# Cross-attention: the value products of a batch packed in one PSUM bank, with one flip per batch; division and row scaling moved to GpSimd

## The reference

```
xn  = layernorm(x)                         # rows scaled: (x - mean) * rstd
q   = rmsnorm_per_head(xn @ Wq.T)          # 32 heads of 8 columns
k   = rmsnorm_per_head(ctx @ Wk.T)
v   = ctx @ Wv.T
p   = softmax(q k^T / sqrt(8))             # per head, 128 x 128
x  += concat_heads(p @ v)
```

## Time and profile before

| | before |
|---|---|
| median of three runs | 487.55 us (486.32 to 487.72) |
| span of the profiled execution | 485.7 us |
| PE busy | 422.1 us (87%) |
| DVE busy | 347.6 us (72%) |
| ACT busy | 175.4 us (36%) |
| POOL busy | 60.0 us (12%) |
| stage C, first scores to first product of stage D | 349.72 to 445.67 us |

### The profile page before, as it was taken

How to read it: one execution, slowest core, us unless ns; L and a number is a source line. 1 busy time by engine, 2 the same in 40 slices (tenths; PEclk the granted TensorE clock), 3 DMA queues, 4 the chain that set the end, 5 groups by cost and what they waited for, 6 DMA issues and landing times.

```text
span 485.7 us, 8153 instructions
## 1 busy us (share of the span) xinstructions
PE 422.1 (87%) x2754; PEld 264.6 (54%) x2754; DVE 347.6 (72%) x948; ACT 175.4 (36%) x230; POOL 60.0 (12%) x132
## 2 busy tenths in 40 slices
PE   5269998999999987999999999999878777596896
PEld 4125554555555543366666667677556555364444
DVE  7895888888887858466545626676876777868693
ACT  1105444455454451233343433343354444341001
POOL 3222324233242110000000000000000000000000
PEclk9777999999999998999999999999998889876997
DMA  6552335466364031000000000233125554630011
GB/s 214 151 164 70 97 118 158 133 216 196 121 197 123 4 118 43 0 2 0 1 0 0 1 1 11 62 90 111 53 78 164 163 160 126 180 89 1 1 43 43
DMA packets 63408, 42.53 MB, mean 88 GB/s; under 512 B 4625, under 2 KB 61201, under 8 KB 63377
## 3 DMA queue, kind: packets, MB, share of 16 engines
q1 hardware_dynamic: 62080, 41.24, 28.4%
q10 hardware_dynamic: 1296, 0.89, 0.7%
HBM read 27.76 MB, written 14.16 MB: 86 GB/s over the span
## 4 chain that ended last, share of the span: by engine, by line
issue 52%; PE 23%; DVE 14%; POOL 4%; DMA 3%; SPq 1%; ACT 1%; POOLq 0%; DVEq 0%
PE psum L501 7%; PE psum L469 3%; PE psum L489 3%; DVE mx L1114 3%; PE psum L456 2%; PE psum L816 2%; POOL parts L315 1%; PE psum L800 1%; DVE stats L1089 1%; PE psum L587 1%; DMA qstk<-mT 1%; DMA wa<-in_wa 1%; PE psum L725 1%; DVE rope_ab L1103 1%; DMA kstk<-stack_scratch 1%
## 5 line engine op out<-in xcount | busy, mean ns | idle before, releaser
L857 ACT ACTIVATE prob<-psum 128x1024 f32<-128x1024 f32 x64 | 65.6, 1024 | 89.8 <-PE psum L489 89.7
L1114 DVE TENSOR_REDUCE mx<-psum 128x2 f32<-128x512 f32 x128 | 84.1, 682 | 17.9 <-PE psum L469 16.9
L1334 DVE SCALAR_TENSOR_TENSOR xall<-psum,comb,xall 128x256 f32<-128x256 f32 x128 | 53.1, 477 | 41.5 <-PE psum L612 41.1
L612 PE MATMUL psum<-wdn,act 128*128 128x256 f32 x320 | 75.5, 379 | 0.6 <-DVE xall L1331 0.6
L599 PE MATMUL psum<-xnT,wup 128*128 128x512 f32 x160 | 76.0, 598 | 0.0
L612 PEld LDWEIGHTS psum<-wdn,act 128*128 128x128 f32 x320 | 60.7, 190 | 25.9 <-issue 19.1
L501 PE MATMUL psum<-prob,vt 128*32 128x256 f32 x512 | 69.0, 389 | 0.7 <-DVE pvT L1128 0.5
L900 ACT ACTIVATE rel<-psum 128x512 f32<-128x512 f32 x40 | 23.9, 597 | 96.2 <-PE psum L599 96.2
L469 PE MATMUL psum<-kstk,qstk 128*128 128x256 bf16 x256 | 50.8, 283 | 3.4 <-DVE mx L1114 3.3
L315 POOL TENSOR_TENSOR parts<-qk_rest,parts 128x512 bf16<-128x512 f32 x15 | 17.3, 1156 | 244.2 <-ACT parts L925 236.5
L958 ACT ACTIVATE prob<-psum 128x1024 f32<-128x1024 f32 x32 | 32.7, 1024 | 31.4 <-PE psum L710 30.4
(11 more groups left out here) (149 smaller groups left out, 484.7 us busy)
## 6 DMA issues: line engine op xcount, KB each, us to landing
qstk<-stack_scratch SPq DMA_DIRECT2D x32, 256.0 KB, 3.2
kstk<-stack_scratch SPq DMA_DIRECT2D x64, 128.0 KB, 3.3
stack_scratch<-parts SPq DMA_DIRECT2D x32, 192.0 KB, 2.3
stack_scratch<-parts SPq DMA_DIRECT2D x32, 128.0 KB, 2.2
wup<-in_wup SPq DMA_DIRECT2D x4, 640.0 KB, 4.8
wdn<-in_wdn SPq DMA_DIRECT2D x4, 640.0 KB, 5.6
stack_scratch<-parts SPq DMA_DIRECT2D x32, 64.0 KB, 1.9
ctx<-in_ctx SPq DMA_DIRECT2D x10, 128.0 KB, 2.2
```

Of the source, the lines that this page charges most:

```text
L612: last = nc.tensor.matmul(y_banks(y)[:, j // 2, (j % 2) * D:(j % 2 + 1) * D], act2[n % 2][:, j * P:(j + 1) * P], wdn[:, BLOCKS[g], :], sta ...
L857: nc.scalar.activation(prob[k % 2][:], exp_buf(k).rearrange("p a n -> p (a n)"), ACT.Exp, scale=SCALE).then_inc(exp_done, 1)
L1114: nc.vector.tensor_reduce(mx[:, half, :, 4 * s + p4:4 * s + p4 + 1], bank.rearrange("n (b m) -> n b m", b=2), AX_X, ALU.max).then_inc(misc ...
L1334: last = nc.vector.scalar_tensor_tensor(out=xall[:, b, :], in0=src, scalar=comb[:, b, e:e + 1], in1=xall[:, b, :], op0=ALU.mult, op1=ALU.add)
```

## The change

In stage C the products of all four steps of a batch go to one PSUM bank (7). Each step owns 128 columns of it; its two groups of four heads (pp 0 and 1) are accumulated onto each other: the pitch of `vt` grows from 32 to 40 columns, the values move to columns 8 to 15, and the second group's weight is read from column 0 and the first's from column 8, so that the two groups' results lie in different rows of the same 32 partitions. The count of matmuls stays. DVE then flips a batch once (`flip_c`), takes the reciprocal of 32 sums at once, GpSimd does the division in four instructions (`divide_c`), and DVE flips back (`flip_back_c`). The flips of batch b-1 now stand in slot b: `flip_c` at spot 0, in front of `v`, and `flip_back_c` at spot 4. PE's wait on `pv_free` stands at step 0 alone. `normalize_c` moves from DVE to GpSimd, with the mean negated beforehand on DVE. `qkT` moves from spot 3 to spot 4 (behind the scores of step 3), `o` from spot 4 to spot 6. The scaling of q and k becomes one instruction of 512 columns. In stage A only the column slices of `vt` change.

```diff
@@ (tiles, semaphores)
-        vt = [sb(f"vt{i}", [P, 2, 16, 32]) for i in range(2)]
+        vt = [sb(f"vt{i}", [P, 2, 16, VROW]) for i in range(2)]        # VROW = 40
+        den_c = sb("den_c", [P, 32])
+        nmean = sb("nmean", [P, NB])
@@ c_uses
             u = [("v",)] if m and spot == 0 else []
-            u += [("qkT",)] if t and spot == 3 else []
-            u += [("o",)] if o and spot == 4 else []
+            u += [("qkT",)] if t and spot == 4 else []
             u += [("xT",)] if pqk and spot == 5 else []
             u += [("cT",)] if pqk and spot == 5 else []
+            u += [("o",)] if o and spot == 6 else []
             u += [("qk",)] if pqk and spot == 7 else []
@@ PE, pv_c
                 pe.wait_ge(exp_done, NB * PAIRS + b * C_STEPS + k + 2)
-                if k % 2 == 0:
-                    pe.wait_ge(pv_free, 2 * NB + 2 * b + k // 2 + 1)
+                if k == 0:
+                    pe.wait_ge(pv_free, 2 * NB + 2 + b)
                 v = vt[par][:].rearrange("m a h r -> m (a h) r")
                 for pp in range(2):
                     for j in range(4):
                         h = 4 * pp + j
-                        g = 2 * (k % 2) + pp
-                        last = nc.tensor.matmul(pv_bank(k // 2)[32 * j:32 * j + 32, g * P:(g + 1) * P],
-                                                v[:, 8 * k + h, :], prob[k % 2][:, h * P:(h + 1) * P],
-                                                start=True, stop=True)
+                        last = nc.tensor.matmul(pv_bank(1)[32 * j:32 * j + 32, k * P:(k + 1) * P],
+                                                v[:, 8 * k + h, 0:32] if pp else v[:, 8 * k + h, 8:40],
+                                                prob[k % 2][:, h * P:(h + 1) * P],
+                                                start=(pp == 0), stop=(pp == 1), skip_group_check=True)
@@ PE, stage D
-            pe.wait_ge(pv_free, 4 * NB + 2)
+            pe.wait_ge(pv_free, 3 * NB + 2)
@@ POOL
-            with pool.Fori(0, 4) as i:
-                for par in range(2):
-                    third(NB + 2 * i + par, par)
+            def normalize_c(b):
+                pool.wait_ge(stats_ready, b // 4 + 1)
+                nc.gpsimd.tensor_scalar(xn[b % 2][:], xall[:, b, :], nmean[:, b:b + 1], rstd[:, b:b + 1],
+                                        ALU.add, ALU.mult).then_inc(xn_ready, 1)
+            def divide_c(b):
+                pool.wait_ge(den_ready, b + 1)
+                pool.wait_ge(o3_ready, NB + b)
...
+                for k in range(4):
+                    last = nc.gpsimd.tensor_tensor(
+                        o[:, k // 2, k % 2], cells[:, k, :, 0:2 * HD].rearrange("p n (t d) -> p n t d", d=HD),
+                        by[:, k].unsqueeze(3).broadcast_to((P, 4, 2, HD)), ALU.mult)
+                last.then_inc(o2_ready, 1)
...
+            for b in range(NB):
+                flags = c_flags(b)
+                if b < NB - 3:
+                    xn_gone(c_base(b - 1) + c_index(c_flags(b - 1), ("xT",)) if b else
+                            B_END + C_PRO.index(("xT", 1)))
+                    normalize_c(b + 3)
+                if b:
+                    divide_c(b - 1)
+                if b < NB - 2:
+                    third(NB + b + 2, b % 2)
+            divide_c(NB - 1)
@@ DVE, c_use("qk")
-                    for ten in range(2):
-                        last = nc.vector.tensor_tensor(
-                            qkn[:, ten].rearrange("n (h d) -> n h d", d=HD),
-                            bank[:, ten * D:(ten + 1) * D].rearrange("n (h d) -> n h d", d=HD),
-                            rs[:, 32 * ten:32 * ten + 32].unsqueeze(2).broadcast_to((P, 32, HD)), ALU.mult)
-                    last.then_inc(misc_free, 1)
+                    nc.vector.tensor_tensor(qkn[:].rearrange("n t (h d) -> n (t h) d", d=HD),
+                                            bank.rearrange("n (h d) -> n h d", d=HD),
+                                            rs[:].unsqueeze(2).broadcast_to((P, 64, HD)), ALU.mult
+                                            ).then_inc(misc_free, 1)
@@ DVE, divide_c(b, i) goes, and in its place
+            def flip_c(b):
+                dve.wait_ge(pv_done, NB * PAIRS + b * C_STEPS + C_STEPS)
+                nc.vector.transpose(pvT[0][:], pv_bank(1)).then_inc(pv_free, 1)
+                dve.wait_ge(pv_free, 2 * NB + b + 3)
+                nc.vector.reciprocal(den_c[:].rearrange("p (x t) -> p x t", t=2),
+                                     pvT[0][:].rearrange("p (x r) -> p x r", r=32)[:, :, 2 * HD:2 * HD + 2]
+                                     ).then_inc(den_ready, 1)
+            def flip_back_c(b):
+                dve.wait_ge(o2_ready, b + 1)
+                nc.vector.transpose(o3[:], o2[:]).then_inc(o3_ready, 1)
@@ DVE, slot_c
-                if pqk:
-                    normalize(b + 3, (b0 + 1) % 2)
                 n = 0
                 for spot in range(2 * C_STEPS):
-                    if spot in (3, 7):
-                        divide_c(b, spot // 7)
+                    if spot == 0 and shape:
+                        flip_c(b - 1)
+                    if spot == 4 and shape:
+                        flip_back_c(b - 1)
@@ DVE, after the slots
+            flip_c(NB - 1)
...
             weigh(0)
+            flip_back_c(NB - 1)
             ring(("o",))
```

More of the change, by code:

```diff
@@ L28 @@
 MAX_ROW = 46
+VROW = 40
 PAIRS = 8
@@ L160, in build @@
         qk_ready = sem("qk_ready")
+        stats_ready = sem("stats_ready")
+        den_ready = sem("den_ready")
+        o2_ready = sem("o2_ready")
         hi_done = sem("hi_done")
@@ L502, in pv @@
                             pv_bank(1)[32 * j:32 * j + 32, (g % 2) * D:(g % 2 + 1) * D],
-                            vt[par][:, mb, 2 * k + s, :],
+                            vt[par][:, mb, 2 * k + s, 8:40],
                             prob[k % 2][:, (2 * s + mb) * D:(2 * s + mb + 1) * D],
@@ L1056, in _, with xn_gone @@
                 slot(b, 0, b)
-            with pool.Fori(0, 4) as i:
-                for par in range(2):
-                    third(NB + 2 * i + par, par)
+            def normalize_c(b):
[5 more added lines that the diff above has]
+                pool.wait_ge(o3_ready, NB + b)
+                cells = pvT[0][:].rearrange("p (k n r) -> p k n r", k=4, r=32)
+                o = o2[:].rearrange("p (i n k t d) -> p i k n t d", i=2, n=4, t=2, d=HD)
+                by = den_c[:].rearrange("p (k n t) -> p k n t", k=4, t=2)
+                for k in range(4):
[3 more added lines that the diff above has]
+                last.then_inc(o2_ready, 1)
+            def xn_gone(u):
+                pool.wait_ge(misc_free, u + 1)
+            for b in range(2):
+                normalize_c(b)
+            xn_gone(B_END + C_PRO.index(("xT", 0)))
+            normalize_c(2)
+            third(NB, 0)
+            third(NB + 1, 1)
+            for b in range(NB):
[9 more added lines that the diff above has]
+            divide_c(NB - 1)
         @block.vector
@@ L1108, in take_values @@
             def take_values(par, bank):
-                return nc.vector.tensor_copy(vt[par][:, :, :, 0:HD],
+                return nc.vector.tensor_copy(vt[par][:, :, :, 8:16],
                                              bank[:, 0:D].rearrange("m (a h d) -> m a h d", a=2, d=HD))
@@ L1145, in _ @@
                 steps.then(nc.vector.memset(vt[i][:], 0.0))
-                last = nc.vector.memset(vt[i][:, :, :, HD:HD + 1], 1.0)
+                last = nc.vector.memset(vt[i][:, :, :, 16:17], 1.0)
                 last.then_inc(pv_free, 1)
@@ L1344, in _ @@
             norm_stats(0, 4)
-            for b in range(2):
-                normalize(b, b)
+            nc.vector.tensor_scalar(nmean[:, 0:4], mv[:, 0:4, 0], -1.0, None, ALU.mult).then_inc(stats_ready, 1)
+            for i in range(2):
+                halves = vt[i][:].rearrange("m a (g t j) r -> m (a g) t j r", g=2, t=2)
+                nc.vector.memset(vt[i][:, :, :, 16:17], 0.0)
+                nc.vector.memset(halves[:, :, 0, :, 24:25], 1.0)
+                nc.vector.memset(halves[:, :, 1, :, 17:18], 1.0)
             def c_use(kind, par, bank, b):
@@ L1371, in c_use @@
                 elif kind == "v":
-                    nc.vector.tensor_copy(vt[par][:].rearrange("m a h r -> m (a h) r")[:, :, 0:HD],
+                    nc.vector.tensor_copy(vt[par][:].rearrange("m a h r -> m (a h) r")[:, :, 8:16],
                                           bank[:, 0:D].rearrange("m (h d) -> m h d", d=HD)).then_inc(misc_free, 1)
@@ L1375, in c_use @@
                     nc.vector.tensor_tensor(rows_of(b), bank[:, 0:D], rows_of(b), ALU.add).then_inc(misc_free, 1)
-            def divide_c(b, i):
-                dve.wait_ge(pv_done, NB * PAIRS + b * C_STEPS + 2 * (i + 1))
-                nc.vector.transpose(pvT[i][:], pv_bank(i)).then_inc(pv_free, 1)
-                dve.wait_ge(pv_free, 2 * NB + 2 * b + i + 3)
```

(15 more changed lines are left out.)

## The result

The changed kernel takes **502.23 us** (median, 500.74 to 504.5), the kernel before beside it 486.94: a ratio of 1.0354, interval 1.0284 to 1.0423. The kernel is slower, as forecast, and by nearly the forecast amount (502.3). The profiled execution has a span of 499.6 us, 13.9 over the one before.

A forecast was written before the change was run, and what follows sets the result against it. Bound: a ring through all engines in stage C's slots, no busy engine. Slot 0 -0.7, slots 1 to 4 +9.3, slot 5 +3.0, tail +3.2 make +14.8: span 500.5, plus 1.85, 502.3 us; range 495 to 509.

The forecast's parts named there:

- The gate: Stage C: PE's first products wait for DVE's flip behind `qk`'s scaling; 14.11 us a slot at full clock, 11.98 before.
- The clock: Stage C: the four steps behind PE's longer stop run partly at 1.2 GHz; 1.1 us a slot, between 0 and 1.9.
- Ends of the stage: Stage C's first and last slots: slot 0 -0.7 us, slot 5 +3.0, slots 6 and 7 up to stage D +3.2.
- Stages A, B and D at nothing: Outside stage C: A and B cost nothing, bound 0.4 us; the last flip and division lie beside D's first products.
- DRAM hidden: Stage C: the transfer across two slots needs 14.3 us a slot, under 15.2, so PE's 0.55 us wait goes.
- GpSimd: Stage C's division on POOL: four products at 0.34 us, 1.35 in all, hidden in some 2.6 us of room.
- rival 2: Stage C: PE's first products not held by the flip; transfer through DRAM gives 12.2 us a slot, 483.9 us; chance 0.07.

## Why the prediction was right, and where it was off

*The gate.* Right, step by step. End of `qk` to first product: 5.74 us measured in slot 4 (404.84 to 410.58), 5.87 forecast. Four steps: 3.81, forecast 2.26 and 1.1 for the clock. `qkT` to `cT`: 2.55, forecast 2.17. `cT` to the end of `qk`: 3.76, forecast 3.81. These are the terms of one slot; together they are its 15.86. The gate alone, in the kernel before, gives 15.33 a slot, and taken out of the change it leaves 0.6% (two banks) or 0.5% (an earlier flip) of 3.5%. The Trainium skill, PSUM — Partial Sum Buffer, "Summary: rules for kernel authors", asks for a different bank; the runs agree that it helps, and show that one bank does as well when its release comes early.

*The clock.* This is the term that was mis-sized: 1.1 us a slot in the sum, 1.75 measured with PE kept busy. I chose between 0 and 1.9 by "today most slots have a slow stretch"; but behind a stop of 4.5 us all four steps were slow in slots 2 and 4, and three of them in slots 1 and 3. The four steps took 3.34, 3.82, 3.54 and 3.81 us, 3.63 on average, for 2.26 + 1.1 = 3.36. The bound of 1.9 for four wholly slow steps was too high for them alone: 3.81 is 1.55 over 2.26. The other part of the miss lies in a term that the sum had at full clock, `qkT` to `cT`: `qkT` and the products behind it are slow too (1.06 and 0.67 to 1.01 us in slots 2 and 4), and it took 2.49 on average for 2.17, where it is 2.09 to 2.25 with PE kept busy. The two parts, +0.27 and +0.32, less 0.07 before the first product, are the 0.5 by which 15.72 exceeds 15.2. With 1.75 a slot would be 15.86 and slots 1 to 4 +11.9 (11.4 measured). In slot 5 the same two parts make 0.5 and 0.4 of the 1.1 us by which it exceeds +3.0. The other 0.3 is arithmetic: what was left for the work behind the rest, 4.70, had been found with slot 4's 2.81 from `qkT` to the rest's end, but slot 5 before had 2.47 there (416.61 to 419.08).

*Ends of the stage.* Slot 0 right to the tenth. The end was 1.1 us dearer than the +3.2, within its bound of 4.4: the steps before the routing ran at the lower clock (rows of 0.85, 1.03, 1.08 and, for `dlg`, 1.89 us, against 1.06 before), which I had counted by half. The routing started 19.93 us after the first transposes (437.52 to 457.45), against 17.31 before: +2.6, where I had taken +1.4; what follows it, +1.7, was forecast at +1.8.

*Stages A, B and D at nothing.* By the profiles -5.2 us, the larger part of it the dear stage D in the profile before. The -1.4 is within the spread of stages that are the same in every kernel here, and the 40.03 before is the longest stage D of all the profiles. The -5.2 cancelled the 4.3 us of underestimate in stage C (2.1, 1.1 and 1.1 in the table; it shows in stage D's first product, at 463.39 us and not near 460), and left the span at +13.9 for +14.8, 499.6 us for 500.5. The profiled execution took 501.43 us, 1.83 above its span, as the 1.85 of the forecast has it; the median of the four runs happens to lie another 0.8 higher, and that gives back what the span lacked.

*DRAM hidden.* Right for the changed kernel: the wait for `kstk` is gone. In every version without the gate PE waits for the transfer again, 1.9 to 5.8 us over slots 1 to 4, and mostly in the long slots. "12.2 per slot" in rival 2 took the shortest distance in the profile (12.78, where 13.47 and 14.78 stood beside it) and left out the lower clock behind the awaited transfer; with one bank 12.5 to 13.4 came.

*GpSimd.* 0.294 us a product and 1.05 for the four, forecast 0.34 and 1.35; row scaling 0.555, hidden as forecast.

*Rival 2 (no gate, 483.9 us)* was not what happened, but its price was fair: 486 to 488 with the gate gone, 483.1 to 483.6 with the end of the stage mended too, which the rival did not have.

## What to carry to other kernels

Taking work off an engine that is not the bound bought nothing that could be measured here; moving an instruction in its written order can cost everything that queues for its result. Before a double-buffered bank is made single, look at what stands in front of the release in the releasing engine's stream, and put the release where that engine waits anyway. Cost work that starts behind a long stop of PE at the lower clock, with what follows the first steps too. Read every instance of a wait before taking its length from one. And when a mended ring does not reach its sum, look for the next ring (here a transfer across two slots) before doubting the mend.

## What the runs showed of the hardware

- A stop of PE of 4.5 us was followed by four steps of 3.34 to 3.82 us in place of 2.16 (rows of 1.03 to 1.08 us for 0.62 to 0.65); filled with matmuls that nothing reads, the steps ran at the upper of the two levels (2.4 GHz). Behind waits of 1.7 and 1.9 us for a transfer, with shorter ones before them, `qk` took 3.5 and 3.6 us for 2.03.
- The way through DRAM was no constant: from POOL's third part to the scores that waited for it were 12.05 to 14.78 us, 12.78 to 14.78 within one profile of the kernel before; PE's longest wait for `kstk` was 1.4 us there and 3.6 in one with an early flip.
- GpSimd's product of 64 columns took 0.294 us on average and its two-input instruction of 512 columns 1.157; the row scaling of 256 columns with one tensor input 0.555. On DVE the four products of 64 columns took 0.63 together, less than four times the 0.22 of a two-input instruction of 64 columns in the reciprocal root.
- Two profiles of one kernel differ by 0.7 us in the mean slot (12.61 and 13.29), and stage D, the same in every kernel here, took 36.1 to 40.0 us; the two ends have granted clocks of 0.96 and 0.85.
